# A transformer block in one kernel: softmax division moved behind the output projection, products in groups of four, PSUM banks by kind of work

## What is computed

```python
def _attention(xq, xkv, wq, wk, wv, wo, bo):
    q, k, v = heads(xq @ wq), heads(xkv @ wk), heads(xkv @ wv)
    attn = softmax(einsum('bihd,bjhd->bhij', q, k) * D_HEAD ** -0.5)
    return einsum('bhij,bjhd->bihd', attn, v).reshape(B, S, D_ATTN) @ wo + bo
h = layernorm(x, ln1);  x = _attention(h, h, sa_...) + x
h = layernorm(x, ln2);  x = _attention(h, cond_emb, ca_...) + x
h = layernorm(x, ln3);  p = h @ ff_w1 + ff_b1
a, gate = p[..., :1024], p[..., 1024:]
return a * gelu(gate) @ ff_w2 + ff_b2 + x
```

## Time and profile before

| | |
|---|---|
| time, median of 3 executions | 1303.99 us (1301.44 to 1304.22) |
| profiled execution, span from first to last instruction | 1301.8 us (no other time is given for it) |
| PE matmul busy | 1251.0 us, 96%, 9417 instructions |
| DVE busy | 862.5 us, 66% |
| POOL busy | 821.7 us, 63% |
| ACT busy | 638.5 us, 49% |
| granted TensorE clock, mean | 0.994 of 2.4 GHz |
| instructions | 23662 |

### The profile page before, as it was taken

The page is one execution under the profiler, slowest core; times in us unless marked ns, Lnnn a source line. Parts: engine busy times, 40 slices in busy tenths (PEclk is TensorE's granted clock), DMA queues, the critical chain, the costliest instruction groups (busy, mean ns, idle before and its releaser), DMA issues.

```text
span 1301.8 us, 23662 instructions
## 1 busy us (share of the span) xinstructions
PE 1251.0 (96%) x9417; PEld 791.9 (61%) x9417; DVE 862.5 (66%) x1145; ACT 638.5 (49%) x922; POOL 821.7 (63%) x443
## 2 busy tenths in 40 slices
PE   4899999999999999999999999999999999889998
PEld 3655555655655655655665654666566666468887
DVE  4667576676676677766765764588788887764433
ACT  3336644544544445654444444447664575434532
POOL 1387787777777777688788779855575654540000
PEclk9999999999999999999999999999999999999999
DMA  3010100100100100100100000012001020000000
GB/s 84 13 34 14 22 2 13 21 1 14 22 1 13 22 1 14 22 1 13 22 1 13 13 7 20 14 44 74 26 17 30 26 62 6 10 5 17 17 10 24
DMA packets 70709, 25.52 MB, mean 20 GB/s; under 512 B 39416, under 2 KB 70600, under 8 KB 70600
## 3 DMA queue, kind: packets, MB, share of 16 engines
q1 hardware_dynamic: 70543, 23.99, 7.7%
q10 hardware_dynamic: 56, 0.01, 0.0%
HBM read 21.62 MB, written 2.10 MB: 18 GB/s over the span
## 4 chain that ended last, share of the span: by engine, by line
PE 88%; ACT 5%; DVE 3%; issue 2%; SPq 1%; DMA 1%; POOL 0%; ACTq 0%; DVEq 0%; POOLq 0%
PE psum L817 24%; PE psum L833 21%; PE psum L700 21%; PE psum L683 8%; PE psum L788 5%; PE psum L842 4%; PE psum L912 3%; ACT z L1152 1%; ACT probs L1235 1%; PE psum L794 1%; DVE m_part L1016 1%; SPq L622 1%; PE psum L865 1%; ACT h_hi L1166 1%; DVE psum L1046 1%
## 5 line engine op out<-in xcount | busy, mean ns | idle before, releaser
L1235 ACT ACTIVATE probs<-psum 128x1024 f32<-128x1024 f32 (+1 forms) x320 | 327.5, 1024 | 440.5 <-PE psum L817 435.7
L1360 POOL TENSOR_TENSOR acc<-acc,probs 128x1024 f32<-128x1024 f32 x192 | 457.3, 2382 | 74.5 <-ACT probs L1235 63.6
L1016 DVE TENSOR_REDUCE m_part<-psum 128x2 f32<-128x1024 f32 x256 | 312.2, 1222 | 212.8 <-PE psum L788 212.5
L1046 DVE RECIPROCAL psum<-psum 128x128 f32<-128x128 f32 x256 | 234.4, 941 | 33.9 <-PE psum L842 33.9
L833 PE MATMUL psum<-probs,val 128*64 128x512 f32 x1024 | 247.9, 605 | 0.0
L1360 POOL TENSOR_TENSOR acc<-probs 128x1024 f32<-128x1024 f32 (+1 forms) x64 | 152.8, 2387 | 123.8 <-ACT probs L1235 122.6
L1365 POOL TENSOR_TENSOR o_lo<-pv_sb,o_hi 128x512 fp32r<-128x512 f32 x64 | 81.8, 1278 | 114.0 <-ACT o_hi L1249 113.5
L833 PEld LDWEIGHTS psum<-probs,val 128*64 128x64 f32 x1024 | 63.2, 136 | 116.3 <-issue 114.5
L817 PE MATMUL psum<-row_max,minus 64*128 64x512 f32 (+1 forms) x640 | 126.8, 391 | 0.0
L817 PE MATMUL psum<-q_hi,k_hi 64*128 64x512 f32 x512 | 116.2, 449 | 6.5 <-ACT probs L1235 4.3
L788 PE MATMUL psum<-k_hi,q_hi 64*128 64x512 f32 x512 | 108.9, 421 | 6.1 <-DVE m_part L1016 4.4
(11 more groups left out here) (148 smaller groups left out, 2206.5 us busy)
## 6 DMA issues: line engine op xcount, KB each, us to landing
row_max<-m_cols SPq DMA_DIRECT2D x256, 0.5 KB, 2.0
xr<-in_x SPq DMA_DIRECT2D x8, 256.0 KB, 3.8
wv_raw<-in_L_xattn_sa_wv SPq DMA_DIRECT2D x8, 256.0 KB, 3.4
wqk_raw<-in_L_xattn_sa_wq SPq DMA_DIRECT2D x16, 128.0 KB, 2.4
wqk_raw<-in_L_xattn_sa_wk SPq DMA_DIRECT2D x16, 128.0 KB, 2.6
wo_raw<-in_L_xattn_sa_wo SPq DMA_DIRECT2D x16, 128.0 KB, 2.1
wqk_raw<-in_L_xattn_ca_wq SPq DMA_DIRECT2D x16, 128.0 KB, 2.3
wo_raw<-in_L_xattn_ca_wo SPq DMA_DIRECT2D x16, 128.0 KB, 2.0
```

The costliest lines, as they stand in the source:

```text
L1016: dve.tensor_reduce(m_part[:, half, :, t, kh], psum[:, bank0:bank0 + 2, :], AX.X, ALU.max).then_inc(s_x_read, 1)
L1046: dve.reciprocal(part, part).then_inc(s_recip, 1)
L1235: act.activation(probs[buffer_of(J, u)][0:plan.ks, :, :], psum[0:plan.ks, SB:SB + 2, :], ACT.Exp, scale=SCALE).then_inc(s_exp, 1)
L1360: pool.tensor_tensor(total, last if kt == 1 else total, now, ALU.add).then_inc(s_acc, 1)
```

## The change

1. **Division behind the projection.** `E` (ACT) writes the high part `o_hi` straight from PSUM, a new `L` (DVE) the low part; `N` and `R` are gone. `D` becomes one step for both halves, four matmul pairs of 32 columns into four groups of 32 rows of bank 5; ACT copies them to SBUF (`copy_d`, `d` in the orders), SP moves them by four DMAs (`move_d`, `T`) into columns `d_cols`, and DVE takes one reciprocal of 128x16 (`B`). As the division is now by head and row, `Y` keeps the two heads in two banks (6 and 7), for each half and each pair of 128-row tiles, and DVE adds them with 16 scalar_tensor_tensor of 128x256 (times `d_cols`, plus `x`).
2. **Rows in another order.** So that the DMAs have contiguous pieces, a tile holds every fourth row. `X` reads its weights at a step of 4 elements (8 in cross), `E` and `L` read PSUM at a step of 4, the first two normalisations write `h` at a step of 4. The row maxima go by 4 DMAs in a self iteration instead of 16; in the cross stage directly by 2, and `M` is gone from PE and DVE. `top` has two buffers.
3. **Groups of four.** `P` takes four units, so a self iteration has four groups instead of eight and a cross iteration one instead of two. `probs` has 12 buffers instead of 8. Half 0 goes to bank 4, half 1 to bank 5, which it shares with `D`.
4. **New orders** of all engines. ACT waits for `s_s` ahead of the two buffer waits in `S`.

```diff
-        self.group = min(2, self.kt)
-        self.probs = 8 if own else 4
+        self.group = 4
+        self.probs = 12 if own else 4
...
-    if kind in "DMc":
-        return (5,) if kind != "M" or not own else ()
+    if kind == "P":
+        return (4 + a,)
+    if kind in "Dc":
+        return (5,)
     if kind == "t":
-        return ((4, 5, 2, 3) if J == 0 else (6, 7, 6, 7) if J >= 3 else (5, 5, 5, 5))[2 * a[0] + a[1]],
+        return ((4, 5, 2, 3) if J == 0 else (6, 7, 6, 7))[2 * a[0] + a[1]],
...
+            def move_d(J):
+                wait_read(sp, ("D", J, 0))
+                if J >= 2:
+                    wait_read(sp, *y_items(J - 2))
+                for half in range(2):
...
+                        sp.dma_start(d_cols[J % 2][:, c0:c0 + 4],
+                                     d_rows[row:row + 1, :].rearrange("o (p t) -> o p t", p=P)).then_inc(s_d_cols, 16)
...
-                        mm = pe.matmul(bank(bank0 + h), q[r, q0:q0 + P], k_hi[r, kh * HALF:(kh + 1) * HALF], start=True, stop=True)
+                        mm = pe.matmul(bank(bank0 + h), q[r, half * HALF + t:(half + 1) * HALF:4], k_hi[r, kh * HALF:(kh + 1) * HALF], start=True, stop=True)
...
-            def D(J, a):
-                plan, prep = plan_of(J), prep_of(("D", J, a))
-                pe.wait_ge(s_acc, A0[J] + (plan.kt - 1) * (a + 1))
-                wait_free(pe, ("D", J, a))
-                for h in range(2):
-                    mm = pe.matmul(psum[h * DH:(h + 1) * DH, prep, :], ones[0:plan.ks, :], acc[a][0:plan.ks, h, :], start=True, stop=True)
+            def D(J):
+                plan, prep = plan_of(J), prep_of(("D", J, 0))
+                pe.wait_ge(s_acc, A0[J + 1])
+                wait_free(pe, ("D", J, 0))
+                for half in range(2):
+                    for h in range(2):
+                        row = d_row(half, h)
+                        mm = pe.matmul(psum[row:row + 32, prep, :], ones[0:plan.ks, :], acc[half][0:plan.ks, h, :], start=True, stop=True)
                 mm.then_inc(s_prep, 1)
             def Y(J, a):
...
+                half, m = a
+                wait_read(pe, ("P", J, half))
+                pe.wait_ge(s_wo_lo, J + 1)
+                wait_free(pe, ("Y", J, a))
+                for t in range(2):
+                    rows = slice((2 * m + t) * P, (2 * m + t + 1) * P)
+                    for i, (o, w) in enumerate(((o_hi, wo_hi), (o_hi, wo_lo), (o_lo, wo_hi))):
+                        for h in range(2):
+                            mm = pe.matmul(psum[:, prep_of(("Y", J, a), h), t * DM:(t + 1) * DM], o[half][rows_of(h), rows], w[rows_of(h), :],
+                                           start=(t == 0 and i == 0), stop=(i == 2), skip_group_check=True)
+                mm.then_inc(s_prep, 1)
...
+            def L(J, a):
+                dve.wait_ge(s_o_hi, 2 * J + a + 1)
+                dve.tensor_tensor(in_tiles(o_lo[a][:]), tiled(psum[:, PVB + a, :]), in_tiles(o_hi[a][:]), ALU.subtract).then_inc(free_of(("P", J, a)), 1)
+
+            def B(J):
+                dve.wait_ge(s_d_cols, 64 * (J + 1))
+                dve.reciprocal(d_cols[J % 2][:], d_cols[J % 2][:]).then_inc(s_recip, 1)
...
+                for h in range(2):
+                    bank = prep_of(("Y", J, a), h)
+                    for t in range(2):
...
+                        op = dve.scalar_tensor_tensor(x, psum[:, bank, t * DM:(t + 1) * DM], d_cols[J % 2][:, c0:c0 + 1], x, ALU.mult, ALU.add)
...
+                    op.then_inc(s_free[bank], 1)
...
             def E(J, a):
                 plan = plan_of(J)
                 act.wait_ge(s_pv, U0[J] + plan.kt * (a + 1))
-                after(act, s_o_lo, 2 * J + a - 1)
-                act.activation(pv_sb[a][:], psum[:, PVB, :], ACT.Copy).then_inc(s_pv_out, 1)
+                if J:
+                    wait_prep(act, ("Y", J - 1, (a, 1)))
+                act.activation(in_tiles(o_hi[a][:]), tiled(psum[:, PVB + a, :]), ACT.Copy).then_inc(s_o_hi, 1)
```

More of the change, by code:

```diff
@@ L87 @@
 K0 = before(lambda p: p.khalf)
-MOVED = before(lambda p: 16 * 8 if p.own else 16 * 2)
+MOVED = before(lambda p: 16 * 2)
 def added(J, u):
@@ L302, in prep_uses, with units_of, items_of @@
     for token in order:
-        item, turn = item_of(*token)
-        banks = prep_banks(*item)
-        if banks and turn == 0:
-            uses[item] = {bank: count[bank] for bank in banks}
-            for bank in banks:
-                count[bank] += 1
-    return uses
-def item_of(kind, J, a):
+        for item, turn in items_of(*token):
+            banks = prep_banks(*item)
+            if banks and turn == 0:
+                uses[item] = {bank: count[bank] for bank in banks}
+                for bank in banks:
+                    count[bank] += 1
+    return uses
+def units_of(J, g):
+    group = plan_of(J).group
+    return range(g * group, (g + 1) * group)
+def items_of(kind, J, a):
     if kind in "KQV":
-        return (kind, J, 0), a
-    if kind == "Y":
-        return (kind, J, a[0]), a[1]
-    return (kind, J, a), 0
+        return [((kind, J, 0), a)]
+    if kind == "P":
+        kt = plan_of(J).kt
+        return [((kind, J, u // kt), 0) for u in units_of(J, a) if u % kt == 0]
+    return [((kind, J, a), 0)]
 def turns(item):
-    return 2 if len(prep_banks(*item)) == 2 else 1
+    return 2 if item[0] in "KQV" and len(prep_banks(*item)) == 2 else 1
 def ends(order, turn_of):
@@ L329, in ends @@
     for token in order:
-        item, turn = item_of(*token)
-        if prep_banks(*item) and turn == turn_of(item):
-            out[item] = len(out)
+        for item, turn in items_of(*token):
+            if item[0] != "P" and prep_banks(*item) and turn == turn_of(item):
+                out[item] = len(out)
     return out
@@ L404, in block_kernel @@
         wo_lo = sb("wo_lo", [P, DM], F32R)
-        pv_sb = [sb(f"pv_sb{a}", [P, HALF]) for a in range(2)]
-        o_hi = sb("o_hi", [P, HALF], F32R)
-        o_lo = sb("o_lo", [P, HALF], F32R)
+        o_hi = [sb(f"o_hi{a}", [P, HALF], F32R) for a in range(2)]
+        o_lo = [sb(f"o_lo{a}", [P, HALF], F32R) for a in range(2)]
+        d_rows = sb("d_rows", [P, HALF])
+        d_cols = [sb(f"d_cols{b}", [P, 16]) for b in range(2)]
         z = sb("z", [P, 4, DM])
         ident = sb("ident", [P, P])
-        ones = sb("ones", [P, DH])
+        ones = sb("ones", [P, 32])
         eps = sb("eps", [P, 1])
@@ L562, in wait_h, with y_items, d_row @@
             wait_read(eng, *[("t", q, (c, k)) for c in chunks for k in range(KD)])
-        def half_before(J, a):
-            return (J, 0) if a else (J - 1, 1)
+        def y_items(J, half=None):
+            return [("Y", J, (a, m)) for a in range(2) if half in (None, a) for m in range(2)]
+        def d_row(half, h):
+            return 32 * (2 * half + h)
         def last_reads(q):
@@ L821, in PV @@
                 plan = plan_of(J)
-                for u in range(g * plan.group, (g + 1) * plan.group):
+                for u in units_of(J, g):
                     half, kt = u // plan.kt, u % plan.kt
                     if kt == 0:
-                        after(pe, s_pv_out, 2 * J + half)
+                        wait_free(pe, ("P", J, half))
                         if half == 0 and J % 2 == 0:
@@ L843, in D @@
                 mm.then_inc(s_prep, 1)
             def Y(J, a):
-                half, turn = a
-                if turn == 0:
-                    pe.wait_ge(s_o_lo, 2 * J + half + 1)
-                    pe.wait_ge(s_wo_lo, J + 1)
-                steps = []
-                for o, w in ((o_hi, wo_hi), (o_hi, wo_lo), (o_lo, wo_hi)):
-                    steps.append(lambda n, t, r, o=o, w=w: (o[r, (2 * n + t) * P:(2 * n + t + 1) * P], w[r, :]))
-                two_banks(("Y", J, half), turn, DM, steps)
+                half, m = a
@@ L901, in down @@
                 if q == 0:
[L902 to L903 removed]
+                    wait_read(pe, *[item for item in PREP_USE if item[0] in "PD" and item[1] == NITER - 1])
                 if n == 0 and f % 4 == 0:
@@ L1060, in Y @@
-                x = xr[:, 8 * b + 4 * half + 2 * m:8 * b + 4 * half + 2 * m + 2, :]
-                dve.tensor_tensor(x, x, psum[:, prep, :].rearrange("p (t d) -> p t d", t=2), ALU.add).then_inc(free_of(("Y", J, half), m), 1)
+                for h in range(2):
+                    bank = prep_of(("Y", J, a), h)
+                    for t in range(2):
+                        tile = 2 * m + t
+                        x = xr[:, 8 * b + 4 * half + tile, :]
+                        c0 = 8 * half + 4 * h + tile
+                        if h and t == 0:
+                            dve.wait_ge(s_y_half, 4 * J + 2 * half + m + 1)
+                        if h and t:
+                            wait_half(dve, ("Y", J, a), 0)
+                        op = dve.scalar_tensor_tensor(x, psum[:, bank, t * DM:(t + 1) * DM], d_cols[J % 2][:, c0:c0 + 1], x, ALU.mult, ALU.add)
+                        if h == 0 and t == 0:
```

(3 more changed lines are left out.)

246 lines of the change are left out of this document (109 added, 137 removed), and 68 rows, old and new, of tables (CROSS_ORDER, OPENING, SELF_ORDER).

## The result

The kernel after takes 1382.9 us (median of 4 runs, 1380.0 to 1387.0) against 1303.4 for the kernel before on the same chip: ratio 1.061, 95% interval 1.059 to 1.063. It is 79 us slower; 1344 was forecast, so the sign held and half of the size. The measured time lies 2 us inside the upper end of the stated range (1385) and 18 above the range of the rival that the forecast rests on (1325 to 1365). The profiled execution spans 1382.5 us, 80.7 more than that of before.

The account below looks back on a forecast made before the run. The length of PE's own list was taken as the bound. Span 1301.8, +31 for self iterations, +13 for cross steps, -4 for opening and end gave 1341.8; with 2.2 from profiled span to median, 1344, range 1270 to 1385.

Parts of the forecast that it names:

- rival D: X's weight loads in both stages: strided reading doubles the load and PE waits, +50 us, 1394 (1370 to 1400); chance 0.13.
- A: The rival used as forecast: gaps between S too short for exp, and DVE late; 1344, 1325 to 1365; chance 0.45.
- The list, -2.8: PE's self list: fewer groups save 1.36, one merged D 1.21, Y 0.2; in all 2.8 us of 49.2.
- Self waits, +4.9: Self iteration: PE waits for exp in short gaps (4.3 us) and for DVE before S10, S14 and S15; iteration 51.3, +2.1.
- The walk: Start times of S0 to S15 in one self iteration, stepped through the lists at the forecast's prices; next S0 at 51.3.
- five short gaps, 4.3 us: Self stage: five gaps between S hold less work than exp's 2.3 us distance; with restarts PE waits 4.3 us an iteration.
- Strided loads, 0: X's weight loads at a step of 4 or 8: bounds 0 and 50 us, taken as 0 because the load has slack.
- Cross, +0.84 a step: Cross step: list from 17.59 to 15.9 without V, plus waits for banks and DVE; mean 19.15, +13 us over 15 steps.
- At nothing: Costs taken as hidden: T's DMAs ahead of M1 (5 us to spare), B, ACT's d, POOL; normalisations' transposes inside the range.
- the -4 for opening and end: The opening's stops for the maxima (2.1) and the end's for o_lo on POOL (2.1 of 2.8) should go: -4 us.
- B: Exp floor alone in the self stage, DVE's Y quick enough, cross winning 0.6 a step: 1313, up to 1325; chance 0.15.
- C: The length of PE's list decides, so the kernel gets faster: 1235 in full, 1270 for half; chance 0.22.

Follow-up runs that it names:

- run 1: The kernel after with X weights read as 128 neighbouring elements again instead of every fourth (eighth in cross): 1373.4 us, ratio 1.051.
- run 3: The kernel after with DVE adding only one column of 256 for the second head in each Y: 1347.3 us, ratio 1.030.
- run 4: The kernel before with the self stage's X weights read at a step of 4 elements: 1314.7 us, ratio 1.005.
- run 7: The kernel after with packed X weights, DVE adding one column of the second head, and exp of one head, together: 1321.8 us, ratio 1.013.
- run 11: As run 7, with DVE's row maxima of the self stage over one head of two as well: 1309.9 us, ratio 1.001.
- run 9: The kernel after with packed X weights and DVE adding one column of the second head, groups of four kept: 1330.8 us, ratio 1.017.
- run 6: The kernel after with exp taking one head of two from the second iteration on: 1379.4 us, ratio 1.058.

## Why the prediction was right in sign and half in size

The forecast span was 40 us longer, the measured one is 80.7 longer. Of the 40.7 between them the cross stage has 25, the self stage 11 and the opening and the end together 4.3.

That 1382.9 lies in the stated range is luck. Its part above 1365 was there for rival D, and D's mechanism costs about 10 us and not 50; A's own range was missed.

**The list, -2.8: right.** `P` gives 0.60, `D` 1.02. The steps into and out of a group cost 1.97 above their pace in the period of before (eight `P`, two `D`) and 1.05 in that of run 1 (four and one): 0.92. In all 2.54; 0.15 + 0.20 is the 0.34 of a group. Only the 0.2 of `Y` did not come (3.20 for 3.03; in run 3, where `Y` hardly waits, 3.05). Four column groups do run side by side: eight instructions take 1.00 where four took 1.01. At that the trace agrees with the four tiles of the Trainium skill (TensorEngine Tiling (Array Packing), Tiling Modes).

**Self waits, +4.9: the mechanism right, the sum by some luck.** The period was forecast 2.1 longer and is 2.7 longer, x15 = 41 of the 42 measured. With the 2.5 that the list saved, waits and longer pieces come to 5.2. The walk holds up to `S13` within 0.3, and within 0.1 at `S5` to `S9`: the distances that exp enforces were priced rightly. But the 5.2 contains the strided loads, 0.67, which the forecast put at nothing; with packed loads (run 1) the period is 51.27, the 51.3 of the forecast. DVE's `Y` was taken as 1.5 and is 1.66 (212.2 / 512 x 4).

What the forecast doesn't tell is how the waits lie above each other. By removal, DVE's `Y` gives 1.46, strided loads 0.67, then exp 0.63 and row maxima 0.84 once the others are away; together 3.5 of the 5.2. Exp by itself gives 0.06. The step "five short gaps, 4.3 us" is right as a distance and wrong as a cause that could be taken away: the 1.8 that the prediction itself read for two `X` was a second floor in the same gaps, and was used for DVE's `Y` only.

**Strided loads, 0: wrong, with a small price.** The load takes 306 ns, not 185. The bound of 50 had every load in the open; run 4 gives 10 in the kernel before, run 1 9.5 in the kernel after. The Trainium skill (SBUF — State Buffer, Door 1) said that each access to a new line pays, and the trace agrees with it, at 306 ns for 185. What the rule can't say is how much of a load lies beside other matmuls: here 0.07 of the added 0.12 us.

**Cross, +0.84 a step: the term that failed.** The stage is 38 us longer for 15 steps, where 13 was forecast. Like steps, with no normalisation near, take 20.1 us without V and 21.1 with it. Before they took 17.58 and 19.03, and 18.7 and 19.6 was forecast: 2.3 more for 0.84. Their idle time is 2.6 and 2.25, so the waits, forecast at 2.5 in the mean, look well priced. What failed is the other side, "from 17.59 to 15.9". By the starts, as in the table, PE's list of such a step goes from 18.31 in the mean to 18.2, not to 16.6:

| like cross steps, mean | D | P and M | Y | X | last piece of S | all else | idle | step |
|---|---|---|---|---|---|---|---|---|
| before | 2.17 | 3.65 | 3.23 | 0.92 | 1.02 | 7.32 | 0 | 18.31 |
| after | 1.00 | 3.58 | 3.30 | 1.65 | 1.32 | 7.32 | 2.43 | 20.60 |
| forecast of the difference | -0.86 | -0.61 | -0.2 | 0 | 0 | 0 | +2.5 | +0.84 |

`X` has loads of 319 ns, longer than its pairs, and the last piece of `S` has the hidden part of the wait behind it. `D` gave more than forecast, but merging `P` and dropping `M` gave almost nothing.

There is a deeper fault behind it: the step was built as a shorter list plus waits, as if each part taken from the list came off the time. With packed loads (run 1) `X` falls by 0.5 in such a step, the idle time rises by as much, and the steps stay at 20.1 and 21.0. So the list doesn't set them here. By the trace the chain does in which PE and DVE hand banks 6 and 7 to each other. That the idle time came out at 2.5 is then partly luck. Run 3 shortens DVE's part of that chain and the steps fall to 18.6 and 20.0, the stage by 11.6 us.

The remaining 24 against before (runs 7 and 11 end at 321 and 323) were not taken apart by a run. In run 11 like steps take 18.46 and 19.83; over 15 steps that is 13 of its 26 us; the rest lies in the steps with a normalisation and at the turn. The trace puts the waits on `Y` behind Q's low parts, 10.0 + 4.0 in run 11, on `Y` behind `Y`, and on the normalisations' transposes behind DVE. At a granted clock of 0.96 a stage of 323 has lost some 13 us, at 0.99 one of 297 has lost 3 (estimates from clock and length), so up to 10 of the 24 may be the clock's; in the kernel after it is 0.98 and so some 4 of the 38. In the kernel after the clock fell to half at 1150.3 and at 1194.7, after stops of PE of 0.61 and 1.20 us; that the stops are the cause is not shown.

**At nothing: right but for the end.** The maxima's DMA costs PE 0.2, `d` and `B` appear in no wait of PE. Of the -4 for opening and end, the opening gave 2.7. The end lost 3.0 instead of gaining: two waits of `Y` for DVE (1.47 and 1.84), and behind them a group that took double:

```profile
1222.83 0.58 PE L865 MATMUL psum<-wo_hi,o_hi 64*128 64x256 f32 x2 [1.84 <-DVE xr L1069]
...
1224.41 7.09 PE L842 MATMUL psum<-probs,cross_val 77*64 77x512 f32 x16
```

The window of that stretch has the clock:

```profile
1224.40:1232.00 7.60, 7.60 (x22) 2.28 (x22) 2.35 (x5) 0.60 (x1) 0.18 (x1) 0.50 0.00 0
```

0.50 of full speed is 1.2 GHz. A group of 3.6 took 7.1, which is more than the 3.0 that the end lost. In run 9, with a shorter `Y` and at 0.99, the whole end takes 157.1 us.

**The rivals.** B (exp alone, DVE's `Y` quick enough) falls with runs 3 and 6, D (50 us of loads) with runs 1 and 4. C, in which the list decides, is nowhere in reach: with four suspects away the kernel is as slow as the one before. A stands in the self stage, with the row maxima added to its floors. The new orders (point 4 of the change) were not tried by themselves.

**The signs.** The two intervals of 2.2, `P` at 3.6, `D` at 1.0 and `K0` and `Y` behind `xr` came. Idle time in the self stage rose from 8 to 38 us and not to 80, and PE's busy time rose by 12 where a fall of 42 was expected, because the profile counts short waits as busy. One sign was badly chosen: intervals of 2.2 together with a load over 0.23 were to mean D. Both came, and D is not the cause.

## What to carry to other kernels

Small pieces of work between two dependent instructions are not only overhead: they hold up every floor of that gap. Before merging them, write down for each gap all minimum distances (here 2.2 by exp, 1.95 by row maxima, and what a shared pair of banks needs to be drained), not only the longest. An experiment that removes one floor measures its distance to the next. And moving work from one long instruction to several that hold a bank costs where the next user of that bank stands, whatever the engine's sum: DVE became less busy (862 to 781 us) and yet the most costly wait.
